# Layer 3's ternary weights turned by DMA as 16-bit copies, and a new order for the work between attention and its feed-forward layer

## The reference, cut to what matters

```
# L2_xattn: 16 heads of 16; attn = fake-quantised softmax(q k^T)
out = einsum('bhqk,bhkd->bhqd', attn, v) -> (B, N, C)
x = x + out @ Wp + bp

# L2_ffn: H2 = 682
def _quantize(w):                       # ternary: -1, 0 or +1
    return clip(round(w / (mean(|w|) + 1e-8)), -1, 1)
h = layernorm(x)
x = x + (sigmoid(h @ q(w1).T) * (h @ q(w2).T)) @ q(w3).T
```

## Time and profile before

| what | before |
|---|---|
| median of 3 runs | 1076.54 us (1074.39 to 1076.83) |
| the profiled execution's own time | 1081.43 us |
| its span, first to last instruction | 1079.7 us |
| mean granted TensorE clock | 0.828 of full speed |
| busy: PE, DVE, ACT, POOL | 884.0, 739.6, 458.2, 141.3 us |
| end of the attention's last `values` | 792.36 us from the span's start |
| first product of `ffn(l2)` | 821.86 us |

### The profile page before, as it was taken

One profiled execution on the slowest core, in us unless ns is written; L12 is line 12 of the kernel. 1 busy time (PEld: TensorE's weight loads), 2 busy tenths in 40 slices (PEclk: granted clock), 3 DMA queues, 4 the chain that ended last, 5 costly groups with the idle time before them and its releaser, 6 DMA issues.

```text
span 1079.7 us, 11762 instructions
## 1 busy us (share of the span) xinstructions
PE 884.0 (82%) x4286; PEld 525.0 (49%) x4286; DVE 739.6 (69%) x974; ACT 458.2 (42%) x695; POOL 141.3 (13%) x222
## 2 busy tenths in 40 slices
PE   5999794489799999998997676777777898878796
PEld 3434562245655555544554333444345566644554
DVE  1775558954567887786687988888843436659773
ACT  2213436642333322121223888988933435422110
POOL 1000000000024334425000111111110000001111
PEclk8899886589989999998999555555577879889898
DMA  9500003100222220420009699787830000000000
GB/s 267 170 0 1 1 0 46 20 3 6 31 32 43 44 39 4 79 37 0 1 10 173 120 162 170 128 136 130 139 50 17 1 0 1 1 1 0 10 10 19
DMA packets 202204, 56.78 MB, mean 53 GB/s; under 512 B 182990, under 2 KB 200484, under 8 KB 202148
## 3 DMA queue, kind: packets, MB, share of 16 engines
q1 hardware_dynamic: 202036, 55.87, 27.7%
q10 hardware_dynamic: 112, 0.17, 0.1%
HBM read 20.62 MB, written 1.05 MB: 20 GB/s over the span
## 4 chain that ended last, share of the span: by engine, by line
PE 52%; DVE 25%; ACT 9%; issue 6%; DMA 6%; ACTq 1%; POOL 1%; POOLq 0%; DVEq 0%; SPq 0%
PE ps L874 48%; DMA arena<-xc 5%; ACT xc L1774 3%; DVE arena L2458 3%; PE ps L452 2%; ACT arena L1784 1%; DVE arena L2090 1%; DVE xn_t L1907 1%; PE ps L1004 1%; DVE sq L2369 1%; DVE sq L2366 1%; DVE arena L2467 1%; ACT arena_split L1691 1%; DVE xc L2262 1%; PE ps L1316 1%
## 5 line engine op out<-in xcount | busy, mean ns | idle before, releaser
L874 PE MATMUL ps<-arena 128*128 128x16 f16 (+7 forms) x1760 | 269.2, 324 | 68.1 <-ACT xc L1774 30.2
L874 PE MATMUL ps<-arena_split 128*128 128x512 f32 (+5 forms) x736 | 205.5, 443 | 25.5 <-DVE arena_split L1928 14.6
L874 PEld LDWEIGHTS ps<-arena 128*128 128x128 f16 (+4 forms) x1760 | 133.0, 130 | 178.7 <-issue 82.0
L874 PEld LDWEIGHTS ps<-arena_split 128*128 128x128 f32 (+5 forms) x736 | 138.0, 201 | 98.0 <-issue 38.1
L2458 DVE TENSOR_REDUCE arena<-ps 128x1 f32<-128x1024 f32 x128 | 152.4, 1221 | 27.8 <-PE ps L874 25.9
L1774 ACT ACTIVATE xc<-ps,arena 128x1024 int16<-128x1024 f32 x128 | 153.2, 1202 | 24.9 <-POOL arena L850 21.1
L874 PE MATMUL ps<-sq,arena 128*64 128x256 f32 (+3 forms) x256 | 80.9, 515 | 8.0 <-DVE sq L2369 7.9
L1558 ACT ACTIVATE act_buf<-ps 128x512 f32<-128x512 f32 (+2 forms) x34 | 20.3, 596 | 98.5 <-PE ps L874 98.5
L850 POOL TENSOR_SCALAR arena<-arena 128x1 f32<-128x1 f32 x128 | 34.0, 265 | 212.9 <-DVE arena L2458 212.9
L822 POOL TENSOR_SCALAR arena<-arena 128x512 f32<-128x512 f32 x12 | 23.1, 1923 | 248.0 <-DVE arena L2284 248.0
L452 PE MATMUL ps<-ident,arena 128*128 128x128 f32 (+4 forms) x194 | 34.5, 324 | 20.7 <-DMA arena<-in_x 6.6
(11 more groups left out here) (279 smaller groups left out, 1299.8 us busy)
## 6 DMA issues: line engine op xcount, KB each, us to landing
arena<-in_L_ffn_w SPq DMA_DIRECT2D x4, 640.0 KB, 6.1
arena_split<-arena_split SPq DMA_DIRECT2D x59, 32.0 KB
arena<-xc SPq DMA_TRANSPOSE x96, 3.3
arena<-in_x SPq DMA_DIRECT2D x1, 1024.0 KB, 5.6
arena<-in_ctx SPq DMA_DIRECT2D x1, 1024.0 KB, 8.1
arena<-in_L_xattn_Wkv SPq DMA_DIRECT2D x2, 512.0 KB, 4.0
arena<-in_L_ffn_gate_w SPq DMA_DIRECT2D x1, 1024.0 KB, 10.0
arena<-in_L_ffn_up_w SPq DMA_DIRECT2D x1, 1024.0 KB, 12.5
```

The costliest lines, as they stand in the source:

```text
L874: return pe.matmul(o, l, r, start=start, stop=stop)
```

## The change

1. The 12 turn groups of `l2` are gone from TensorE, ACT and DVE.
2. POOL, as soon as `weights_fixed` is 2, copies the three ternary weights to 16-bit tiles (`ternary_16`), padding with zeros, and only then writes the zeros of `k3`. `bias_split` now counts 2 after the copies and 3 after the zeros.
3. SP issues three DMA transposes of 1536 16-bit elements per partition each (into `ternary_back`), ahead of those of the keys.
4. ACT, after the attention and once the last `values` are done, copies `ternary_back` into `wt_l2`: four copies (1280, 84, 1280 and 84 elements per partition) ahead of the norm's square, and one of 1536 behind it, which raises `weights_fixed` to 3. TensorE waits for that before `ffn(l2)`.
5. `out_projected` of half 0 moves in front of the last three `values`; its residual moves in front of `tile_out` of the last tile.
6. The norm of half 0 (`l2`) runs ahead of half 1's projection: mean, then `out_turned(1)`, variance, first half of the projection, `ln_rows`, second half; `out_added(1)` moves behind `ln_low`.
7. DVE waits for the three transposes before it writes the second half's quantised queries, which share bytes with `w16`.

```diff
--- before.py
+++ after.py
@@ -256,6 +256,7 @@
         bias_parts = c2([2, D], BF16, parts=96)
         bias_ones = c2([P], BF16, parts=96)
         assert c2.at / 256 <= 92
+        w16 = Cut(88)([6, D], BF16)
         wp2 = hid_buf[:, 1, :].rearrange("p (k n) -> p k n", k=KC)
         assert c.at / 256 <= late_at
         c2 = Cut(0)
@@ -386,6 +387,17 @@
             f()
             marks[name] = (first, len(groups))
 
+        def halves(w):
+
+            flat = w.rearrange("p a b -> p (a b)").bitcast(BF16)
+            return flat[:, 0:6 * D], flat[:, 6 * D:12 * D]
+
+        w2_16, w3_16 = halves(w_l2[0])
+        w1_back, w2_back = halves(w_l2[1])
+        w3_back = w_l2[2].rearrange("p a b -> p (a b)").bitcast(BF16)[:, 0:6 * D]
+        ternary_16 = [w16.rearrange("p a b -> p (a b)"), w2_16, w3_16]
+        ternary_back = [w1_back, w2_back, w3_back]
+
         def tokens_turned(nat, dst, wait):
             for h in range(TH):
                 for k in range(KC):
@@ -410,7 +422,6 @@
             turns = [(NE, P, k * P, mu_nat[:, k, :, :].rearrange("p f k -> p (f k)")) for k in range(KC)]
             groups.append((turns, [(mu_t[0:NE, :].unsqueeze(1), NE, 0, 256, 256)], (load["mu"], 16 * 6), 0))
         mark("small", small)
-        mark("l2", lambda: three(w_l2, wt_l2, H2, None, 2))
 
         def lx():
             turn_in(D, lx_nat[0], lx_t[0], (load["l3x"], 16 * 5), 0)
@@ -716,6 +727,10 @@
                                      allow_slow_non_contiguous=True).then_inc(load["l2w"], 16)
 
             sp.wait_ge(bias_split, 2)
+            for src, dst in zip(ternary_16, ternary_back):
+                sp.dma_start_transpose(dst.rearrange("p (a b) -> p a b", b=P), src).then_inc(load["l2"], 16)
+
+            sp.wait_ge(bias_split, 3)
             for h in range(TH):
                 sp.wait_ge(k_split, h + 1)
                 if h == 0:
@@ -837,8 +852,19 @@
             step(pool.tensor_copy(bias_parts[64:65], bias_rest))
             pool.sem_inc(bias_split, 1)
 
+            pool.wait_ge(weights_fixed, 2)
+            full = H2 // P
+            for w, o in zip(w_l2[0:2], ternary_16[0:2]):
+                o = o.rearrange("p (a b) -> p a b", b=D)
+                step(pool.tensor_copy(o[:, 0:full], w[:, 0:full]))
+                step(pool.tensor_copy(o[0:H2 % P, full], w[0:H2 % P, full]))
+                step(pool.memset(o[H2 % P:P, full], 0.0))
+            o = ternary_16[2].rearrange("p (k n) -> p k n", k=KC)
+            step(pool.memset(o[:, :, H2:], 0.0))
+            step(pool.tensor_copy(o[:, :, 0:H2], w_l2[2]))
+            pool.sem_inc(bias_split, 1)
+
             pool.wait_ge(moe_srm, 2 * NF)
-            pool.wait_ge(weights_fixed, 2)
             step(pool.memset(k3[:, :, :, :, 3, :].rearrange("p i h j d -> p (i h j) d"), 0.0))
             pool.sem_inc(bias_split, 1)
 
@@ -1336,12 +1362,10 @@
                                             o_tok[:, 4 * h + j, k * P:(k + 1) * P], ident[:, :])
                     last.then_inc(ot_turned, 1)
 
-            def out_projected(h, banks):
-                pe.wait_ge(ot_copied, 2 * h + 2)
-                for o in range(KC):
-                    for k in range(KC):
-                        last = mm(ps[:, banks[o], :], wp2[:, k, o * P:(o + 1) * P], o_t[:, k, tok(h)],
-                                  k == 0, k == KC - 1)
+            def out_projected(h, o, bank):
+
+                for k in range(KC):
+                    last = mm(ps[:, bank, :], wp2[:, k, o * P:(o + 1) * P], o_t[:, k, tok(h)], k == 0, k == KC - 1)
                 last.then_inc(att_done, 1)
 
             for u in range(UNITS + VALUES_LAG):
@@ -1353,23 +1377,25 @@
                     out_turned(0, (4, 5))
                 if 3 <= u < UNITS + 3 and by_pe(u - 3):
                     probs_turned(u - 3)
+                if u == UNITS + 3:
+                    pe.wait_ge(load["l2x"], 16)
+                    pe.wait_ge(att_exp, UNITS - 1)
+                    pe.wait_ge(ot_copied, 2)
+                    for o in range(KC):
+                        out_projected(0, o, o)
                 for v in values_after(u):
                     values(v)
 
-            pe.wait_ge(load["l2x"], 16)
-            pe.wait_ge(att_exp, UNITS - 1)
-            out_projected(0, (0, 1))
+            ln_mean_of("l2", 0)
             pe.wait_ge(att_o_used, TT)
             pe.wait_ge(att_exp, UNITS)
             out_turned(1, (2, 3))
-            ln_mean_of("l2", 0)
-            out_projected(1, (6, 7))
-            pe.wait_ge(x_ready, 2 * LN["l2"] + 2)
-            pe_turn(pe, "l2", (0, 2))
             ln_var_of("l2", 0)
+            pe.wait_ge(ot_copied, 4)
+            out_projected(1, 0, 6)
             ln_rows_of("l2", 0)
-            pe_turn(pe, "l2", (1, 2))
-            evacuated(pe, marks["l2"][1])
+            out_projected(1, 1, 7)
+            pe.wait_ge(weights_fixed, 3)
             ffn(l2)
 
             pe_turn(pe, "lx")
@@ -1789,11 +1815,18 @@
                     exponentials(u)
                 if u >= 4 and copied_by_act(u - 4):
                     probs_copy(u - 4)
+            act.wait_ge(load["l2"], 16 * 8)
+            act.wait_ge(att_v, UNITS)
+            full = H2 // P
+            for dst, src in zip(wt_l2[0:2], ternary_back[0:2]):
+                v = src.rearrange("p (r k j) -> p k r j", k=KC, j=P)
+                act.activation(dst[:, :, 0:full * P].rearrange("p k (r j) -> p k r j", j=P), v[:, :, 0:full], ACT.Copy)
+                act.activation(dst[:, :, full * P:], v[:, :, full, 0:H2 % P], ACT.Copy)
             ln_sq_of("l2", 0)
-            copy_out(act, "l2", False, (0, 2))
+            act.activation(wt_l2[2].rearrange("p c (k j) -> p c k j", j=P),
+                           ternary_back[2].rearrange("p (k c j) -> p c k j", k=KC, j=P), ACT.Copy).then_inc(weights_fixed, 1)
             ln_sd_of("l2", 0)
             ln_high("l2", 0)
-            copy_out(act, "l2", False, (1, 2))
             ffn(l2, ACT.Sigmoid)
 
             copy_out(act, "lx", False)
@@ -2313,6 +2346,8 @@
 
             def query_piece(h, i):
 
+                if h == 1 and i == 2:
+                    dve.wait_ge(load["l2"], 16 * 8)
                 v = q_tok[:, 4 * h:4 * h + 4, :].rearrange("p t (h d) -> p (t h) d", d=HD)
                 if i == 0:
                     scaled(v, A["sq"].rearrange("p t h -> p (t h)"), h, 1)
@@ -2473,8 +2508,8 @@
                     TS(o_t[:, k, tok(h)], ps[:, banks[k], :], A["sv"][:, k:k + 1], None, ALU.mult).then_inc(ot_copied, 1)
 
             def out_added(h, banks):
-                dve.wait_ge(att_done, h + 1)
                 for o in range(KC):
+                    dve.wait_ge(att_done, 2 * h + o + 1)
                     last = STT(x_t[:, o, tok(h)], ps[:, banks[o], :], A["bpp"][:, o:o + 1], x_t[:, o, tok(h)],
                                ALU.add, ALU.add)
                     if o == 0:
@@ -2499,16 +2534,14 @@
                     tile_out(u // HEADS - 1)
                 if u == UNITS + 2:
                     out_copied(0, (4, 5))
+            out_added(0, (0, 1))
             tile_out(TT - 1)
-            out_added(0, (0, 1))
+            ln_xc_of("l2", 0)
             out_copied(1, (2, 3))
-            ln_xc_of("l2", 0)
-            out_added(1, (6, 7))
-            copy_out(dve, "l2", True, (0, 2))
             ln_diag_of("l2", 0)
             ln_xn_of("l2", 0)
             ln_low("l2", 0)
-            copy_out(dve, "l2", True, (1, 2))
+            out_added(1, (6, 7))
             ffn(l2, gate_std)
 
 
```

## The result

In four timed runs each, the changed kernel took 1066.83 us (median; 1062.73 to 1067.97) and the kernel before 1076.68 us: so the medians lie 9.9 us or 0.9% apart. The ratio of all these runs is 0.989, with a 95% interval of 0.9863 to 0.9917. It needn't agree with the medians (0.989 of the kernel before is 11.8 us less). The forecast of the median was 1062.4 us, a gain of 14.1 us, with a range of 1057.5 to 1069.5. The profiled executions lie 13.5 us apart (1081.43 and 1067.97 us).

A forecast was written before the change was run, and what follows sets the result against it. The end of layer 3's attention was taken as bound by a chain of waits, one engine after another, up to `ffn(l2)`. Terms -16.2 + 1.9 - 1.1 + 1.3 = -14.1 us gave a median of 1062.4 us, range 1057.5 to 1069.5.

The forecast's parts named there:

- The chain from the last `values`: From the last `values` to the first product of `ffn(l2)`: 29.5 us become 13.3, minus 16.2 us.
- The square root and the diagonal: In half 0's norm: ACT's `w3` copy and table load release the root at 7.25 us; diagonal done at 8.5.
- ACT's copies of `w1` and `w2`: Ahead of the norm's square: 3.0 us, fitting into ACT's 3.3 us wait for `ln_xc` with 0.2 us to spare.
- The table load: Ahead of the norm's square root: 1.28 us with no drain; the skill page's rule would add 1.38 us.
- The projection ahead of the last `values`: Half 0's projection at the full clock, 3.60 us, makes the last `values` end 1.9 us later; 4.9 at half clock.
- The start of the feed-forward block: First 16 records of `ffn(l2)` take 4.4 us instead of 5.55 at the full clock: minus 1.1 us.
- POOL's casts: In layer 2, casts hold up DVE operations that TensorE waits on: two at 0.65 us, plus 1.3; bounds 0 to 4.5.
- The DMA transposes: Three on SP from about 542, issued by 549 and down by 555, ahead of the keys' at 564.3: no cost.
- A: Rival, 15%: the clock stays low in projections, norm and feed-forward start; gain only 6.2 us, 1070.3 us.
- B: Rival, 8%: ACT's copies cost up to twice the row, making ACT the bound; gain 9.8 us, 1066.7 us.
- C: Rival, 2%: the feed-forward block is bound by something else, such as layer 4's weights; no change, 1076.5 us.
- D: Rival, 2%: each POOL cast stops DVE for its whole length; at 5 ns an element 6.8 us slower, 1083.3 us.

The follow-up runs named there:

- order only: The kernel before with the new order of projections, residuals and norm, TensorE's 36 turns kept, no casts or DMA transposes; 1071.68 us, ratio 0.9937.
- casts later: The changed kernel with POOL's casts waiting until DVE has made the hidden product of unit 14; 1064.53 us, ratio 0.9881.
- `w3` behind the root: The changed kernel with ACT's copy of `w3` behind the norm's square root instead of ahead of its table load; 1065.02 us, ratio 0.9884.
- both: The changed kernel with POOL's casts behind DVE's product of unit 14 and ACT's copy of `w3` behind the square root; 1061.94 us, ratio 0.9863.
- both again: The changed kernel with POOL's casts moved later and ACT's `w3` copy behind the square root, timed a second time; 1063.6 us, ratio 0.9875.
- `ln_rows` first: The changed kernel with POOL's casts later, `w3` copied behind the square root, and `ln_rows` ahead of both halves of the second projection; 1067.23 us, ratio 0.9897.
- casts twice: The changed kernel with each of POOL's five casts done two times, same result; 1064.93 us, ratio 0.9884.
- the weights alone: The changed kernel's weights turned by DMA and copied by ACT, with attention's end, projections and norm in the order of before; 1073.18 us, ratio 0.9951.

## Why the prediction was right

The direction and the way were right, and the sum came out at 13.5 us in the traces where 14.1 were forecast. That is in part luck, since three terms were mis-sized, by +1.3, +1.6 and -2.5 us, and these nearly cancel. The gain in the medians, 9.9 to 12.3 us, is under the forecast and inside its range.

- *The chain from the last `values`* was to fall from 29.5 to 13.3 us. It fell to 14.55: 1.2 us less gain. The square root and the diagonal came when forecast (8.56 us behind the last `values`, forecast 8.5). What was missed is `ln_rows`: it starts 0.4 us later, behind the projection's first half, and at half clock it delays what follows by 0.8 us more. The clock fell to 0.50 in the midst of this chain in every profile of the changed kernel (805.8 to 808.5 here), behind a wait of 1.5 us and the 16 one-column records of the variance. ACT's copies of `w1` and `w2` fitted ahead of the square with 0.69 us to spare, forecast 0.2. The table load had no drain behind it (803.40 + 1.28 = 804.68, root at 804.70): the row was right, not the Trainium skill's page "ScalarE: Activation LUTs", section "What ACT_TABLE_LOAD costs".
- *The projection ahead of the last `values`* was to cost 1.9 us at this mark, with the full clock. Without the 1.45 us by which everything stood later already (`out_copied(0)` starts at 789.05 against 787.60), it cost 3.5: the projection took 5.38 us. This is the failed step. I argued that the clock would be at 1.00 because it was in the trace of before and because TensorE would be busier. But in all three profiled executions of this kernel it was still at 0.50 when the projection began. In six others (order only, casts later, `w3` behind the root, both, both again, `ln_rows` first) it was at 1.00 and the projection took 3.68 us, and in casts twice it came halfway (4.66 us). `w3` behind the root has the changed kernel's instructions up to this place:

```profile
792.62 3.68 PE L900 MATMUL ps<-arena,hid_buf 128*128 128x512 f32 x8
```

  So neither value follows from the order of work; the argument from one trace was no argument. With the full clock the term is 1.4 us (6.16 us from the start of `out_copied(0)` to the end of the last `values`, against 4.76 before), so the rest of the sum was sound here.
- *The start of the feed-forward block* was to win 1.1 us. It won 3.57 up to the variance of layer 4's first norm, which stands inside `ffn(l2)`: 38.65 us instead of 42.22, at a mean granted clock of 0.96 instead of 0.84. The first 16 records have 1.63 of it; the rest is half-clock stretches further on that I had not priced:

```profile
811.89:850.54 38.65, 32.13 (x127) 22.64 (x127) 19.39 (x26) 15.31 (x23) 4.27 (x2) 0.96 0.07 21
```

  The same stretch before:

```profile
821.86:864.08 42.22, 35.79 (x127) 25.48 (x127) 17.71 (x24) 15.46 (x24) 0.00 (x0) 0.84 0.00 1
```

  With the weights alone, the block started behind a long wait of TensorE again and took 42.37 us. In every version with both parts it took 38.6 to 41.0, and 43.0 with the order alone. The first 16 records took 3.92 us in all of them but `ln_rows` first (4.25). The rest is less firm: where the block took 40.8 to 40.9 us (casts twice, casts later, `w3` behind the root), the code behind it took 210.5 to 212.4, and 213.6 to 215.8 where it took 38.6 (but `ln_rows` first had 41.0 and 215.7).
- *POOL's casts* were to cost 1.3 us and cost 1.12, by one full collision (0.80 us) and a small one (0.31), where two of 0.65 were priced; the later casts took 0.7 of it back. The Trainium skill, page "SBUF — State Buffer", section "SBUF: two separate sides", has the shared ports as a lock for a whole instruction. The trace agrees, with L2301 at 2.03 us and POOL's cast at 1.27 instead of 0.39, and the doubled casts show that it binds whoever comes second. The casts themselves took 1.25 us for 1280 elements, 0.98 ns an element and so under the lower bound of 1.2.
- *The DMA transposes* were hidden, as forecast: issued in 6.36 us from 542.51, landed 4.0 to 5.2 us each, and the keys' transposes started at 565.4, behind the same work as before.

The sum of the parts in this pair of traces: -14.95 + 3.53 + 1.12 - 3.57 = -13.9, and 0.33 us of drift ahead of the marks, -13.5.

Of the rivals, A (low clock) came in part, in the projection and in `ln_rows`, and what it took was given back by the clock later. B, ACT as the new bound, didn't. C and D didn't.

*Why the medians differ from the traces.* The same instructions take different times. From the variance of layer 4's first norm to the end, where no version differs, the profiles have 215.6 (before), 215.7, 213.6 and 215.8 (changed kernel), 212.4 (casts later) and 208.1 us (both, again); the others lie between. At 212.4 the mean granted clock was 0.91, at 215.6 it was 0.89. This spread of up to 8 us is larger than most parts of the change. The comparison by stages is the sharper one, and 12.3 us, found twice, is the best figure for the whole. The first timing's 9.9 is within its interval of it.

*Open:* what sets the clock at the projection, and whether the 1.4 to 3 us of the best version are more than the 0.7 us of the casts, and whether doubled casts cost time that four runs can't resolve.

## What to carry to other kernels

A wait that is removed is worth what the chain behind it then waits for, so write out the new chain to its end, every engine in it, before adding up what left. When two edits shorten the same stretch, test each alone: here 8.2 and 8.5 us made 11.4, or 13.4 with the projection at a like clock. A collision between two engines that is moved can turn up again behind the place you look at, so follow it to the next common mark. Price TensorE's work at both clocks wherever a trace shows both, take neither from a single execution, and judge small parts by the stretch they are in, not by the whole.

## What was not expected of the hardware

The granted clock at the same place in the same instruction stream differed between executions: the projection took 5.30 to 5.38 us in three of the changed kernel, 4.66 in one and 3.68 in the six named above. At one place two engines that meet on SBUF lost less when one had more to do (POOL's casts doubled: L2304 1.22 us, against 2.03), though they lost more behind it. And a one-input DVE step, L2341 with the casts doubled, was stretched from 0.69 to 1.40 us beside POOL's filling of `k3` with zeros, which reads nothing; L2339 with the casts later took 1.73 us beside a cast.
